# Self-attention layer: the softmax shift of four query tiles turned by one transpose instead of four

## What is computed

```
xf = x.reshape(b, n, c)                       # b = 4, n = 4096, c = 256
f = xf @ Wf + bf                              # keys,    32 wide
g = xf @ Wg + bg                              # queries, 32 wide
hh = xf @ Wh + bh                             # values, 256 wide
scores = jnp.einsum('bnd,bmd->bnm', g, f)
attn = jax.nn.softmax(scores, axis=-1)
o = jnp.einsum('bnm,bmc->bnc', attn, hh)
out = gamma * (o @ Wo + bo) + xf
```

## Time and profile before

| what | us |
|---|---|
| median of three runs | 4612.71 |
| lowest, highest | 4612.49, 4617.48 |
| profiled execution, its own time | 4614.35 |
| profiled execution, from first to last instruction (span) | 4612.5 |
| layer 1, from its first matmul at 2613.6 to the end | 1998.9 |

### The profile page before, as it was taken

One profiled execution on the slowest core, in us unless ns is written; L12 is line 12 of the kernel. 1 busy time (PEld: TensorE's weight loads), 2 busy tenths in 40 slices (PEclk: granted clock), 3 DMA queues, 4 the chain that ended last, 5 costly groups with the idle time before them and its releaser, 6 DMA issues. The chain is left out here.

```text
span 4612.5 us, 78966 instructions
## 1 busy us (share of the span) xinstructions
PE 4354.9 (94%) x24064; PEld 3103.5 (67%) x24064; DVE 3792.9 (82%) x7231; ACT 3344.9 (73%) x5828; POOL 3674.1 (80%) x3475
## 2 busy tenths in 40 slices
PE   5899999999999999999999799999999999999998
PEld 3555556565656565655555488887888788878887
DVE  4899999999999999999999477777777677777775
ACT  5888898989888988898988255555555555555555
POOL 4898989899989989898989277777777677767776
PEclk7899999999999999999999799999999999999999
DMA  2011111111111111111110400022001300040000
GB/s 84 15 45 39 44 40 43 39 46 39 46 38 46 39 46 36 48 34 50 34 50 23 145 20 21 22 77 68 22 15 34 110 21 22 22 123 18 18 21 19
DMA packets 139379, 198.12 MB, mean 43 GB/s; under 512 B 18459, under 2 KB 106501, under 8 KB 138757
## 3 DMA queue, kind: packets, MB, share of 16 engines
q1 hardware_dynamic: 139012, 193.76, 13.3%
HBM read 114.02 MB, written 79.69 MB: 42 GB/s over the span
## 5 line engine op out<-in xcount | busy, mean ns | idle before, releaser
L1292 POOL TENSOR_TENSOR pl<-probs,ph 128x512 fp32r<-128x512 f32 x1024 | 1321.2, 1291 | 572.7 <-ACT probs L1508 289.4
L748 POOL TENSOR_TENSOR dec<-dt,rates 128x384 f32<-128x384 f32 x1536 | 1514.6, 1018 | 240.1 <-ACT dt L634 184.5
L1506 ACT ACTIVATE ph<-ps_s 128x512 fp32r<-128x512 f32 x1024 | 614.9, 601 | 813.2 <-PE ps_s L1388 803.3
L1519 DVE TENSOR_REDUCE part_max<-ps_m 128x1 f32<-128x512 f32 x1024 | 688.9, 688 | 355.9 <-PE ps_m L1371 352.4
L1397 PE MATMUL ps_o<-ph,vh 128*128 128x512 f32 x2048 | 810.0, 396 | 0.1
L1397 PE MATMUL ps_o<-ph,vl 128*128 128x512 f32 x2048 | 806.9, 394 | 0.0
L1547 DVE TENSOR_TENSOR ps_a<-probs,ps_a 128x512 f32<-128x512 f32 x992 | 682.0, 688 | 48.1 <-ACT probs L1508 40.6
L1405 PE MATMUL ps_o<-pl,vh 128*128 128x512 f32 x2048 | 635.5, 391 | 0.0
L1508 ACT ACTIVATE probs<-ps_s 128x512 f32<-128x512 f32 x1024 | 608.6, 594 | 0.0
L906 DVE SCALAR_TENSOR_TENSOR psS<-u,bc,psS 128x384 f32<-128x384 f32 x1024 | 596.9, 610 | 1.2
L915 DVE SCALAR_TENSOR_TENSOR y_tok<-psS,bc,y_tok 128x384 f32<-128x384 f32 x960 | 552.0, 604 | 4.5
(11 more groups left out here) (168 smaller groups left out, 7517.8 us busy)
## 6 DMA issues: line engine op xcount, KB each, us to landing
values_d<-hid SPq DMA_DIRECT2D x64, 512.0 KB, 4.3
xf<-in_x_dram SPq DMA_DIRECT2D x128, 128.0 KB
xb<-in_x_dram SPq DMA_DIRECT2D x128, 128.0 KB
residual_d<-xb SPq DMA_DIRECT2D x32, 512.0 KB, 2.7
vh<-values_d SPq DMA_DIRECT2D x32, 512.0 KB, 6.5
vl<-values_d SPq DMA_DIRECT2D x32, 512.0 KB, 8.4
res<-residual_d SPq DMA_DIRECT2D x32, 512.0 KB, 3.4
out_dram<-res SPq DMA_DIRECT2D x128, 128.0 KB
```

The lines of the kernel that those rows point to most:

```text
L748: last = nc.gpsimd.tensor_tensor(dec[:, q % RING, j - 1, :], dt[:, par, d, token_of(d, j), :], rates[:, d, n, :], ALU.mult)
L1292: nc.gpsimd.tensor_tensor(pl[:, m % DEPTH, :], probs[:, m % DEPTH, :], ph[:, m % DEPTH, :].bitcast(F32), ALU.subtract).then_inc(pl_ok, 1)
L1506: nc.scalar.activation(ph[:, m % DEPTH, :], ps_s[m % 2][:, :], ACT.Exp).then_inc(ph_ok, 1)
L1519: nc.vector.tensor_reduce(part_max[:, qt, kc:kc + 1], ps_m[r % 2][:, :], AX.X, ALU.max).then_inc(max_out, 1)
```

## The change

`shift_hl` held a table of 128 x 128 for each of the four query tiles, with the high part in column 96 and the rest in column 97, and each was transposed by a matmul of its own into its own 128 columns of `ps_m[0]`. After the change there is one table of 128 x 128: query tile q has its parts in columns 96 + 2q and 97 + 2q. One transpose turns it, into columns 0 to 127 of `ps_m[0]`, where rows 96 + 2q and 97 + 2q now hold the parts of tile q. `shift_rows` no longer copies. It multiplies: rows 96 to 127 of those 128 columns, read four times over, times `own_rows`, which is 1 where row r belongs to query tile q and 0 elsewhere, read with each number repeated over 128 columns. So in `gq` each tile's columns have their shift in rows of their own and zeros in the others, and `f_st` has ones in rows 96 to 103. `own_rows` is made once, in the prologue, by a reduction of 32 x 8 numbers of the identity to 32 x 4, with a semaphore of its own.

```diff
-        shift_hl = sb("shift_hl", [P, QT, P])
+        shift_hl = sb("shift_hl", [P, P])
+        own_rows = sb("own_rows", [P, QT])
...
+        rows_ok = sem("rows_ok")
...
-            nc.gpsimd.memset(shift_hl[:, :, :], 0.0).then_inc(const_ok, 1)
+            nc.gpsimd.memset(shift_hl[:, :], 0.0).then_inc(const_ok, 1)
             pool.wait_ge(const_ok, 2)
-            nc.gpsimd.memset(f_st[96:98, :, :].bitcast(F32), 1.0).then_inc(const_ok, 1)
+            nc.gpsimd.memset(f_st[96:96 + 2 * QT, :, :].bitcast(F32), 1.0).then_inc(const_ok, 1)
...
                 pe.wait_ge(max_ok, 4 * c + 3)
-                for qt in range(QT):
-                    mm = pe.transpose(ps_m[0][:, qt * P:(qt + 1) * P], shift_hl[:, qt, :], ident[:, :])
-                mm.then_inc(bcast_ok, 1)
+                pe.transpose(ps_m[0][:, 0:P], shift_hl[:, :], ident[:, :]).then_inc(bcast_ok, 1)
...
-                row, hi, lo = ps_t[:, 0:QT], shift_hl[:, :, 96], shift_hl[:, :, 97]
+                row, hi, lo = ps_t[:, 0:QT], shift_hl[:, 96:96 + 2 * QT:2], shift_hl[:, 97:97 + 2 * QT:2]
...
                 dve.wait_ge(bcast_ok, c + 1)
-                nc.vector.tensor_copy(gq[par][96:P, :], ps_m[0][96:P, :]).then_inc(max_ok, 1)
+                nc.vector.tensor_tensor(gq[par][96:P, :].rearrange("p (q n) -> p q n", q=QT),
+                                        ps_m[0][96:P, None, 0:P].broadcast_to([32, QT, P]),
+                                        own_rows[96:P, :, None].broadcast_to([32, QT, P]), ALU.mult).then_inc(max_ok, 1)
...
             for r in range(KEYS):
                 reduce_max(0, r)
+            nc.vector.tensor_reduce(own_rows[96:P, :], ident[96:P, 96:96 + 2 * QT].rearrange("p (q k) -> p q k", q=QT),
+                                    AX.X, ALU.add).then_inc(rows_ok, 1)
+            dve.wait_ge(rows_ok, 1)
             dve.wait_ge(const_ok, 3)
             shift_parts(0)
             shift_rows(0, 0)
```

## The result

The changed kernel takes 4603.2 us (median of 9 runs, 4597.92 to 4606.9) against 4612.71 for the kernel before (9 runs, 4611.57 to 4620.66). The ratio is 0.9976, with a 95% interval of 0.9967 to 0.9984: by the medians 9.5 us less, by the ratio 11.1, with 7.4 to 15.2 in the interval. The forecast was 10.7 us, 4602.0.

The account below looks back on a forecast made before the run. The prediction took TensorE's cadence in steady chunks as the bound. 10.2 us from 31 chunks, 0 for the product and 0.5 from the prologue make 10.7 us, so 4612.7 becomes 4602.0 us, range 4599.6 to 4606.5.

Parts of the forecast that it names:

- The bound: In steady chunks TensorE's own cadence sets the time; whatever leaves its queue leaves the span; other engines have 25% or more spare.
- Term 1: Steady chunks: three transposes fewer on TensorE in each of 31 chunks, 0.328 us each chunk, 10.2 us in all.
- the bounds: Gain per chunk: 0.48 us if the remaining transpose were free, 0.25 if it took a full matmul's place.
- half-gain: Rival: the remaining transpose keeps up to a full matmul's 0.23 us; 8.3 us gained in all, 4604.4 us; chance 0.16.
- The doubt about the slower matmuls: Behind the transposes matmuls run 0.23 to 0.24 us instead of 0.226; whether one transpose causes it too was left open.
- Term 2: VectorE's product replacing the copy: 0.70 to 1.40 us, hidden before the scores of m = 30, so taken as 0 cost.
- the threshold of 2.80 us: Product length from which TensorE's scores of m = 30 would wait; rival that it runs so slowly, 4626.5 us at 3.5: chance 0.03.
- Term 3: Prologue: 0.7 us saved on transposes less 0.2 for the new reduction, 0.5 us gained.
- The turns: Image turns: trigger and waiter both move forward 0.33 us, so the first wait keeps its length and all 31 chunks count.
- one of the prediction's own signs: The prediction is wrong if stalls at the image turns change by more than 2 us.
- a rival: Stalls at image turns grow and the clock falls there: 1.6 to 2.6 us given back, 4603.6 to 4604.6; chance 0.09.
- The sum: Whole kernel: 10.2 us from steady chunks plus 0.5 from the prologue, 10.7 us gained, 4602.0 us.

Follow-up runs that it names:

- four-alike run: The changed kernel with its one transpose issued four times into the same place: 4617.47 us, ratio 1.0003 to the kernel before the change.

## Why the prediction was right

**The bound.** "TensorE's own cadence sets the time" held: a chunk shortened and lengthened with what TensorE's queue lost or got (0, 1, 4, 10 transposes: 60.21, 60.38, 60.70, 61.35 us), and the four-alike run took the gain back with all else left as changed.

**Term 1** was 0.328 us for each of 31 chunks, 10.2 us. The chunk shortened by 0.35, 10.8 us. Of this 0.32 are the three steps (0.107 to 0.108 each, measured by adding them), and about 0.03 is between the kernel before and the four-alike run (60.73 to 60.70). These differ in the table, the places written to, the product and the ones, and which of these it is was not tested; the prediction did not have it. The choice between the bounds was right: with no transpose at all 0.17 more is gained, so the remaining one does not take a full matmul's 0.23 (half-gain falls, 0.35 and not 0.25 in a chunk) and is not free. The doubt about the slower matmuls is settled: one transpose causes them too, and they are in the 0.17.

**Term 2** at nothing was right in size and in cover: 697 ns, and the threshold of 2.80 us is borne out as far as two points can do it, since 2.16 us cost nothing at the scores and 3.62 us cost 1.02 in every chunk. That the DVE queue takes up the time of the product held as well: with three products VectorE is still idle for 1.92 us before its copy of the sums. What the prediction did not look for is a delay behind the inner loop's jump back, which came at six places with three products; in the changed kernel VectorE's copy is late in this way at the outer jump alone, by 1.35 us.

**Term 3** was 0.5 and came out at 0.45: 0.64 for the transposes and 0.19 for the reduction.

**The turns.** The waits kept their places, as argued. That "the wait keeps its length" was said of the first, where 2.70 us became 2.58, and 3.04 in the other profile. By one of the prediction's own signs, stalls at the turns that change by more than 2 us, it would be wrong all the same: 11.7 us of waits became 9.4, and 16.7 us lost became 12.5. The sign was drawn too tight. The time lost varies from run to run of one kernel by as much as was taken there for a rival, 12.5 us in one profile of the changed kernel and 20.1 in the other. It is this that made the profiled span fall by 16.4 us and not by 11.

**The sum** was 10.7 us. The ratio gives 11.1 and that of the changed kernel run again 9.7 (0.0021 x 4615.93), each within about 4 us either way. The whole time alone would thus not tell the forecast from the half-gain's 8.3 us, and that the first came within half a microsecond of 10.7 is in part luck; the chunk lengths, which repeat to 0.01 us, are what bears the sum out.

## What to carry to other kernels

When one engine is busy without a gap, each instruction on it costs its step in the stream, not its duration: a transpose shown with 272 ns costs 108, and the last one left costs 170 with its edge. Read the step from a merged row (length of the group less that of one, over the number less one), and check it by issuing the thing several times more. Where work moves to an engine with slack, find the place at which it is next waited for, since that gives the threshold, and look at how the runs of one kernel differ among themselves before putting a whole difference of two profiles down to an edit. Gaps at rare places, here three turns, may be worth as much as a saving in every chunk.

## What was not expected of the hardware

A transpose leaves a trace behind itself: for one as for ten, the matmul behind it looks 0.08 us longer and the next is late, 0.06 us beyond the step in all. TensorE's waits at the turns differ in price beyond their length: some are followed by matmuls at the lower of the two clock levels, 0.2 us more each, 11 of them in one execution of the changed kernel and 31 in another. Behind the wait of 4.57 us in the first the granted clock is 0.50 (3619.2 to 3624.0), behind its wait of 2.58 us it is 1.00 (3131.5 to 3134.5). Length alone does not decide it: one of 2.16 us was followed by slow matmuls in the four-alike run, one of 2.87 us was not in the run without a transpose. An engine can start late behind a loop's jump back although it stood idle, VectorE by up to 1.0 us behind the inner jumps with three products, and by 0.12 at the same copies in the changed kernel. And a wait that is removed can uncover the one it hid: the jump back of 5 us had covered 3.3 us of waiting for the queries.
